# Moving one dt projection of a selective scan behind B's transposes, and giving VectorE two tiles of three groups of the last combine

## The chip, the cores and the metric

The kernel runs on one core of one Trainium2 chip. The metric is the time of one execution on the device, in microseconds (us), as the median of three runs.

## The reference

A macaron block on 16 sequences of 256 tokens with 128 features (4,096 tokens): half a mixture of experts (64 experts, the best 3 for each token, at most 64 tokens per expert), a selective scan (SSM) layer, and half a mixture of experts again with the same weights. Cut to what matters:

```python
x = x + 0.5 * ffn(layernorm(x))
x = x + ssm_layer(layernorm(x))
x = x + 0.5 * ffn(layernorm(x))

def ssm_layer(x):
    raw, gate = split(x @ W_in)
    h = silu(conv(raw, conv_w) + conv_b)
    ts, B, C = split(h @ W_x, [64, 80])
    dt = softplus(ts @ W_dt + b_dt)
    dA = exp(dt[..., None] * -exp(A_log))
    dBu = dt[..., None] * B[:, :, None, :] * h[..., None]
    state = dA_t * state + dBu_t          # over 256 times, 256 channels x 16 states
    y = sum_n(state * C)
    return ((y + h * D) * silu(gate)) @ W_out

def ffn(x):
    # gates of the best 3 experts; y = gelu(x w1 + b1) w2 + b2 of each expert's tokens
    out[token] += gate_k * y[row of (token, k)]    # k = 0, 1, 2
```

## The kernel before

All work is in float32 on tiles of 128 partitions. X, the tokens, stays in SBUF as 32 tiles of 128 tokens by 128 features. The order on each engine is written out by hand; engines wait for each other through semaphores that count events (wait(e, "dt", n) waits for the n-th dt).

**Scan.** The sequences are taken in eight blocks (q = 0 to 7) of two sequences. A block has 16 steps (n), one for each set of 32 channels by 4 state slots. For step n TensorE forms dBu by 64 small matmuls (dbu, L931), two steps ahead; ScalarE forms exp(dt·A) four steps ahead (decays, L1176); VectorE runs the recurrence (scan, L1307, three state buffers); GpSimd multiplies the states by C (times_c, L1386, seven product buffers); TensorE sums the products over the states (sum_states, L953). Between these steps the same queues do the work of other blocks: f = q + 2 is the front block, b = q + 1 the one behind it.

The front block's dt comes about so. x_parts (ScalarE, n = 11) copies ts and B, C out of PSUM. dt_proj(f, 0) and dt_proj(f, 1) (TensorE, L900, at n = 12) project ts to the two halves of 128 channels, into PSUM banks 6 and 7. softplus_rest(f, h) (ScalarE, L1132, L1134, L1136; n = 12 and 13) takes the absolute value, exp and ln. dt(f, 0) is formed by VectorE (L1292) at n = 15, dt(f, 1) at n = 0 of the next block. GpSimd's dtu (L1393) multiplies dt by h at n = 0 and 1 of the next block, each ahead of the product of that step. b_transposes(f) (TensorE, L889, n = 13) turns B, bt_copy(f) (ScalarE, L1143, n = 14) copies it to BT, and diagonal (VectorE, L1274, steps 0 and 1 of the next block; GpSimd L1401 and ScalarE L1160 too) spreads it to diagonal blocks for dbu. gates(b, 0) and gates(b, 1) (TensorE, L866, n = 15) write PSUM banks 6 and 7 again, and so wait for dt(f, 0) and dt(f, 1).

At q = 6 and 7 there is no front block. The blocks 0 and 1 of data are prepared ahead of the loop, in an order of its own that the change does not touch.

**Combine.** After the experts, y rows are read back from DRAM into YK by SP's queue, in PIECES of tiles, one read for each k (L394). TensorE multiplies each tile's rows by a diagonal of gates (gate_sums, L597, three k into one PSUM region), four tiles a group. The diagonals are formed by ScalarE among the experts (gate_diagonals, L424). In the second layer the fourth tile of each group is VectorE's instead (moe_residual, L743, three operations that depend on each other), and VectorE adds TensorE's three tiles to X (L748). SP stores X in OUT_PIECES.

## Time and profile before

| | us |
|---|---|
| median of 3 runs | 805.7 (802.46 to 810.35) |
| the profiled execution | 804.58 |
| its span, first to last instruction | 802.8 |
| busy in the span: TensorE, VectorE, ScalarE, GpSimd | 669.5, 595.5, 445.8, 490.5 |
| scan stretch | about 247 to 596 |
| combine of the second layer, reads issued to end | 775.1 to 802.8 |

The views that the prediction reads are these. The waits: for each engine and line, what ended its idle time, the total, how often and the longest. The timeline: instructions in order of time, neighbours of one line merged into a row. The chain: the work that ended last, followed back from the end. In a row of the timeline an instruction's name is the engine and the line of the kernel; neighbours of one engine overlap by up to 0.1 us, since the next starts before the end of the one before is recorded.

### The profile page before, as it was taken

Reading aid. Unit: us, or ns where it says so; the run is one execution under the profiler, and the core shown is the slowest. Engines: PE = TensorE matmul, PEld = TensorE weight load, DVE = VectorE, ACT = ScalarE, POOL = GpSimd, SP = SyncE. Lnnn points to the kernel's source line nnn. Section 1 sums busy time; section 2 is a strip of 40 time slices with the busy share of each in tenths; the row PEclk is TensorE's granted clock in tenths of the full one; section 3 lists DMA queues with packets and bytes.
Section 4 is the critical chain, followed back from the end, with each engine's and each line's share of the span. In section 5 each row is a group of like instructions: output and inputs, shape, how many; then the busy total and the mean of one; then the engine's idle time right before and its main releaser. Section 6 shows DMA issues by size and latency. Waiting matters only on the chain. (4 is left out here: it accounts for less than half of the span.)

```text
span 802.8 us, 27810 instructions
## 1 busy us (share of the span) xinstructions
PE 669.5 (83%) x11782; PEld 401.7 (50%) x11782; DVE 595.5 (74%) x1014; ACT 445.8 (56%) x925; POOL 490.5 (61%) x308
## 2 busy tenths in 40 slices
PE   6728989997978889989898989989989159999957
PEld 2615545555654445454454545454547035555547
DVE  7793443452698999999999999989999954434425
ACT  2400544452787888879798887877634004433420
POOL 3004555551038899999999999999961015555520
PEclk8758999999997999999999999999999579999979
DMA  8995898735283434453524245442009707997538
GB/s 271 397 341 172 290 315 308 234 112 213 117 185 80 98 103 112 124 120 96 147 53 122 73 122 121 123 108 56 4 3 341 288 10 265 323 330 248 168 114 320
DMA packets 87397, 141.07 MB, mean 176 GB/s; under 512 B 9779, under 2 KB 35005, under 8 KB 86000
## 3 DMA queue, kind: packets, MB, share of 16 engines
q1 hardware_dynamic: 82864, 126.99, 51.3%
q0 software_dynamic: 4416, 12.39, 4.1%
q8 instruction: 90, 1.47, 0.8%
q14 instruction: 27, 0.22, 0.1%
HBM read 112.02 MB, written 27.57 MB: 174 GB/s over the span
## 5 line engine op out<-in xcount | busy, mean ns | idle before, releaser
L1386 POOL TENSOR_TENSOR BIG<-BIG,R 128x1024 f32<-128x1024 f32 x127 | 305.5, 2440 | 12.4 <-DVE BIG L1307 12.2
L1307 DVE TENSOR_TENSOR_SCAN BIG<-BIG,ps 128x1024 f32<-128x1024 f32 x128 | 285.3, 2268 | 13.6 <-PE ps L931 10.9
L931 PE MATMUL ps<-BIG,stack 64*32 64x128 f32 x8192 | 155.9, 280 | 30.3 <-DVE BIG L1307 26.4
L931 PEld LDWEIGHTS ps<-BIG,stack 64*32 64x32 f32 x8192 | 118.5, 108 | 107.9 <-DVE BIG L1307 78.6
L767 POOL DMA_INDIRECT R<-xn_dram,tok_idx x64 | 65.4, 1021 | 89.9 <-DVE row_idx L700 70.9
L781 POOL DMA_INDIRECT y_dram<-BIG,row_idx x64 | 64.8, 1013 | 85.3 <-DVE BIG L724 41.7
L1176 ACT ACTIVATE BIG<-R,An 128x510 f32<-128x510 f32 x128 | 84.2, 710 | 5.2 <-DVE BIG L1307 5.1
L415 ACT ACTIVATE BIG<-BIG 128x512 f32<-128x512 f32 x64 | 40.2, 628 | 80.5 <-DVE BIG L716 69.7
L1176 ACT ACTIVATE BIG<-BIG,An 128x510 f32<-128x510 f32 x128 | 83.7, 708 | 0.2
L724 DVE COPY BIG<-ps 128x128 f32<-128x128 f32 x64 | 18.4, 288 | 82.7 <-remote 53.2
L409 ACT ACTIVATE BIG<-ps 128x128 f32<-128x128 f32 x64 | 17.0, 265 | 106.5 <-PE ps L533 71.7
L570 PE MATMUL ps<-BIG 128*64 128x128 f32 x960 | 70.2, 282 | 4.9 <-issue 4.9
L709 DVE COPY BIG<-ps 128x512 f32<-128x512 f32 x64 | 44.0, 688 | 35.5 <-PE ps L543 17.2
L953 PE MATMUL ps<-BIG,fold 128*32 128x512 f32 x512 | 69.4, 610 | 0.0
L543 PE MATMUL ps<-BIG 128*64 128x512 f32 x240 | 66.2, 630 | 0.8 <-ACT BIG L409 0.8
L553 PEld LDWEIGHTS ps<-ident,BIG 128*128 128x128 f32 x256 | 35.8, 209 | 53.7 <-issue 39.1
L570 PEld LDWEIGHTS ps<-BIG 128*64 128x64 f32 x960 | 53.8, 138 | 10.1 <-issue 5.8
L716 DVE TENSOR_TENSOR BIG<-ps,b1T 128x512 f32<-128x512 f32 x64 | 44.0, 688 | 13.3 <-remote 8.4
L1393 POOL TENSOR_TENSOR state_more<-state_more,BIG 128x512 f32<-128x512 f32 x16 | 26.4, 1648 | 43.5 <-DVE state_more L1292 43.5
L553 PE MATMUL ps<-ident,BIG 128*128 128x128 f32 x256 | 48.2, 311 | 1.5 <-DVE BIG L709 1.5
L424 ACT ACTIVATE BIG<-ident,gate 128x128 f32<-128x128 f32 (+1 forms) x112 | 38.0, 386 | 0.0
L1286 DVE SCALAR_TENSOR_TENSOR BIG<-ps,vcol,BIG 128x506 f32<-128x506 f32 (+2 forms) x48 | 34.8, 739 | 3.0 <-ACT BIG L1096 1.7
(184 smaller groups left out, 967.4 us busy)
## 6 DMA issues: line engine op xcount, KB each, us to landing
BIG<-in_L_ffn_w SPq DMA_DIRECT2D x120, 512.0 KB
BIG<-y_dram SPq DMA_DIRECT2D x18, 512.0 KB, 8.8
BIG<-dt_dram SPq DMA_DIRECT2D x32, 256.0 KB, 4.7
R<-c_dram SPq DMA_DIRECT2D x32, 256.0 KB, 7.2
R<-dt_dram SPq DMA_DIRECT2D x32, 256.0 KB, 5.0
y_dram<-zeros SPq DMA_DIRECT2D x3, 2048.0 KB, 16.9
y_dram<-zeros SPq DMA_DIRECT2D x24, 256.0 KB, 5.9
xn_dram<-R POOLq DMA_DIRECT2D x2, 2048.0 KB, 11.3
```

The source lines that it names most:

```text
L543: last = nc.tensor.matmul(ps[a * CAP:(a + 1) * CAP, 1 + s % 2, :], xt[s % 2][:, a * CAP:(a + 1) * CAP], w1s[b][:, a, :], start=True, stop= ...
L553: last = nc.tensor.transpose(ps[:, 3 + s % 2, c * P:(c + 1) * P], hs[s % 2].rearrange("n (p c) -> n c p", c=HC)[:, c, :], ident[:, :])
L570: last = nc.tensor.matmul(ps[a * CAP:(a + 1) * CAP, 5 + s % 2, 0:D], hT[s % 2][:, c, a * CAP:(a + 1) * CAP], w2s[b][:, a, c, :], start=Fal ...
L709: nc.vector.tensor_copy(hs[s % 2], ps[:, 1 + s % 2, :]).then_inc(S("hs"), 1)
L716: nc.vector.tensor_tensor(hb[s % 2].rearrange("p (c n) -> p c n", n=CAP), ps[:, 3 + s % 2, :].rearrange("p (c n) -> p c n", n=CAP), bias, ...
L767: nc.gpsimd.indirect_dma_start(xg[s], None, xn_dram[f], bass.IndirectOffsetOnAxis(tok_idx[:, j:j + 1].bitcast(U32), 0), bounds_check=T - 1 ...
L781: nc.gpsimd.indirect_dma_start(y_dram[f], bass.IndirectOffsetOnAxis(row_idx[:, j:j + 1].bitcast(U32), 0), yo[s], None, bounds_check=K * T ...
L931: last = nc.tensor.matmul(ps[CW * slot:CW * slot + CW, 2 * (st % 2) + b, :] .rearrange("p (g k s) -> p k g s", g=2, k=4)[:, k], dT[q % 2][ ...
L953: last = nc.tensor.matmul(ps[CW * j:CW * j + CW, 4 + h, :], fold32[:, :], prod[(st + j) % RP][:, :, g, :], start=False, stop=(gp == 1 and ...
L1176: last = nc.scalar.activation(dA[:, st % 6, :, g, 1:SEQ], dtR[h][:, j, :].rearrange("p (b t) -> p b t", b=2)[:, :, 1:SEQ], ACT.Exp, scale= ...
L1307: nc.vector.tensor_tensor_scan(state[st % 3], dA[:, st % 6].rearrange("p b g t -> p (b g t)"), ps[:, u:u + 2, :].rearrange("p b n -> p (b ...
L1386: nc.gpsimd.tensor_tensor(prod[st % RP], state[st % 3].rearrange("p (b g t) -> p b g t", b=2, g=2), Cf[q % 2][:, 2 * gp:2 * gp + 2].rearra ...
```

## The change

Two edits in the scan's order. TensorE issues dt_proj(f, 1) at step 14, behind dbu of that step, instead of at step 12. ScalarE copies B's transposes at step 13 and takes the second softplus at step 14, which were the other way round. What VectorE and GpSimd do at which step stays.

Three in the combine of the second layer. In groups 1, 3 and 5 VectorE takes the third tile too (BY_VECTOR), so TensorE has two there, and ScalarE forms no diagonals for them. For such a group VectorE first does k = 0 and 1 of both tiles and then adds TensorE's sum. The last eight tiles of y are read in two pieces of four (PIECES, in both layers), which is three DMA issues more on SP in each layer.

```diff
-PIECES = [(0, 4), (4, 8), (8, 16), (16, 24), (24, 32)]
+PIECES = [(0, 4), (4, 8), (8, 16), (16, 24), (24, 28), (28, 32)]
+BY_VECTOR = [(3,) if g % 2 == 0 or g == 7 else (2, 3) for g in range(8)]
+def vector_tiles(groups):
+    return sum(len(BY_VECTOR[g]) for g in range(groups))
...
-                if f == 1 and s % 4 == 3:
+                g = s // 4 + (2 * r if type(r) is int else 2)
+                if f == 1 and s % 4 in BY_VECTOR[g]:
                     return
...
-            tiles = 4 if f == 0 else 3
+            tiles = 4 if f == 0 else 4 - len(BY_VECTOR[g])
             if g == 0:
-                e.wait_ge(*S.at("gdiag", K * (NI if f == 0 else NI // 4 * 3)))
+                e.wait_ge(*S.at("gdiag", K * (NI if f == 0 else NI - vector_tiles(8))))
...
             for k in range(K):
-                if k:
-                    e.wait_ge(*S.at("x4", K * g + k))
-                nc.vector.scalar_tensor_tensor(out=X[:, i, :], in0=YK[:, k, i, :], scalar=gate[:, i, k:k + 1],
-                                               in1=X[:, i, :], op0=ALU.mult, op1=ALU.add).then_inc(S("x4"), 1)
-                if k == 0:
+                for m, t in enumerate(mine):
+                    i = 4 * g + t
+                    if k:
+                        e.wait_ge(*S.at("x4", K * vector_tiles(g) + len(mine) * (k - 1) + m + 1))
+                    nc.vector.scalar_tensor_tensor(out=X[:, i, :], in0=YK[:, k, i, :], scalar=gate[:, i, k:k + 1],
+                                                   in1=X[:, i, :], op0=ALU.mult, op1=ALU.add).then_inc(S("x4"), 1)
+                if k == len(mine) - 1:
                     e.wait_ge(*S.at("sum", g + 1))
-                    t = X[:, 4 * g:4 * g + 3, :].rearrange("p i d -> p (i d)")
-                    nc.vector.tensor_tensor(t, t, ps[:, g % 4, 0:3 * D], ALU.add).then_inc(S("x"), 1)
+                    t = X[:, 4 * g:4 * g + mine[0], :].rearrange("p i d -> p (i d)")
+                    nc.vector.tensor_tensor(t, t, ps[:, g % 4, 0:mine[0] * D], ALU.add).then_inc(S("x"), 1)
...
# TensorE, in the loop over steps
                             dt_proj(f, 0)
-                            dt_proj(f, 1)
                     if n == 13:
                         if run:
                             sum_states(q, 1, 0, 1)
                         if front:
                             b_transposes(f)
+                    if n == 14 and front:
+                        dt_proj(f, 1)
...
# ScalarE, in the loop over steps
                     if n == 13 and front:
+                        bt_copy(f)
+                    if n == 14 and front:
                         softplus_rest(f, 1)
-                    if n == 14 and front:
-                        bt_copy(f)
```

## Rows read from the trace of the kernel before

**Rows 1.** The waits, 250 to 597 us: engine, line, releaser, total, times, longest

```profile
DVE BIG L1307 <- PE ps L931: 10.9, 8, 2.3
```

**Rows 2.** Timeline of VectorE, block q = 2 and its end: start, length, instructions

```profile
367.87 6.63 DVE L1307 TENSOR_TENSOR_SCAN BIG<-BIG,ps 128x1024 f32<-128x1024 f32 x3
...
376.10 2.29 DVE L1307 TENSOR_TENSOR_SCAN BIG<-BIG,ps 128x1024 f32<-128x1024 f32 x1 [1.60 <-PE ps L931]
...
381.08 0.67 DVE L1292 SCALAR_TENSOR_TENSOR state_more<-ps,state_more 128x512 f32<-128x512 f32 x1
381.66 1.48 DVE L1274 TENSOR_TENSOR BIG<-fold,BT 128x1024 f32<-128x1024 f32 x1
383.07 2.27 DVE L1307 TENSOR_TENSOR_SCAN BIG<-BIG,ps 128x1024 f32<-128x1024 f32 x1
```

**Rows 3.** Timeline of TensorE, same stretch, and a lone projection (L861) later

```profile
372.92 1.98 PE L900 MATMUL ps<-BIG,Wdt 65*128 65x512 f32 x4
...
374.83 1.16 PE L931 MATMUL ps<-BIG,stack 64*32 64x128 f32 x64
...
377.27 2.33 PE L931 MATMUL ps<-BIG,stack 64*32 64x128 f32 x128
...
396.10 1.13 PE L861 MATMUL ps<-R,Wr 128*128 128x512 f32 x2
397.16 1.50 PE L931 MATMUL ps<-BIG,stack 64*32 64x128 f32 x64
```

**Rows 4.** Timeline of GpSimd, same stretch

```profile
363.68 14.03 POOL L1386 TENSOR_TENSOR BIG<-BIG,R 128x1024 f32<-128x1024 f32 x6
378.47 2.37 POOL L1386 TENSOR_TENSOR BIG<-BIG,R 128x1024 f32<-128x1024 f32 x1 [0.77 <-DVE BIG L1307]
...
382.02 3.36 POOL L1386 TENSOR_TENSOR BIG<-BIG,R 128x1024 f32<-128x1024 f32 x1
```

**Rows 5.** Timeline of GpSimd, blocks 6 and 7

```profile
544.53 51.58 POOL L1386 TENSOR_TENSOR BIG<-BIG,R 128x1024 f32<-128x1024 f32 x22
```

**Rows 6.** The chain that ended last, its end: start, length, what

```profile
786.70 12.34 PE ps L597 x108
799.06 0.56 DVE X L748
```

**Rows 7.** Timeline of ScalarE, block q = 2: first softplus's start, the second's passes

```profile
374.08 0.60 ACT L1132 ACTIVATE state_more<-ps 128x512 f32<-128x512 f32 x1 [1.57 <-PE ps L900]
...
377.13 0.58 ACT L1132 ACTIVATE state_more<-ps 128x512 f32<-128x512 f32 x1
...
378.41 0.63 ACT L1136 ACTIVATE state_more<-state_more 128x512 f32<-128x512 f32 x1
```

**Rows 8.** Timeline of VectorE, scans 12 and 17 of blocks 0 and 5

```profile
276.67 6.63 DVE L1307 TENSOR_TENSOR_SCAN BIG<-BIG,ps 128x1024 f32<-128x1024 f32 x3
...
291.40 2.27 DVE L1307 TENSOR_TENSOR_SCAN BIG<-BIG,ps 128x1024 f32<-128x1024 f32 x1
...
504.86 6.63 DVE L1307 TENSOR_TENSOR_SCAN BIG<-BIG,ps 128x1024 f32<-128x1024 f32 x3
...
519.59 2.27 DVE L1307 TENSOR_TENSOR_SCAN BIG<-BIG,ps 128x1024 f32<-128x1024 f32 x1
```

**Rows 9.** Timeline of GpSimd and VectorE, diagonals ahead of the scan

```profile
228.09 4.74 POOL L1401 TENSOR_TENSOR BIG<-fold,BT 128x1024 f32<-128x1024 f32 x2 [5.09 <-PE ps L597]
...
228.81 2.27 DVE L1274 TENSOR_TENSOR BIG<-fold,BT 128x1024 f32<-128x1024 f32 x1
```

**Rows 10.** Timeline of SP and VectorE, combine of the second layer

```profile
775.09 8.13 SPq L394 DMA_DIRECT2D BIG<-y_dram  x15
...
789.01 0.56 DVE L748 TENSOR_TENSOR X<-X,ps 128x384 f32<-128x384 f32 x1 [1.49 <-PE ps L597]
789.48 1.00 DVE L743 SCALAR_TENSOR_TENSOR X<-BIG,gate,X 128x128 f32<-128x128 f32 x3
...
799.53 0.73 DVE L743 SCALAR_TENSOR_TENSOR X<-BIG,gate,X 128x128 f32<-128x128 f32 x2
```

More of the change, by code:

```diff
@@ L736, in moe_residual @@
         def moe_residual(e, S, f, g):
-            i = 4 * g + 3
+            mine = BY_VECTOR[g]
             e.wait_ge(G(f"yk{PIECE[g]}"), 16 * K * (f + 1))
             for k in range(K):
-                if k:
-                    e.wait_ge(*S.at("x4", K * g + k))
-                nc.vector.scalar_tensor_tensor(out=X[:, i, :], in0=YK[:, k, i, :], scalar=gate[:, i, k:k + 1],
-                                               in1=X[:, i, :], op0=ALU.mult, op1=ALU.add).then_inc(S("x4"), 1)
-                if k == 0:
+                for m, t in enumerate(mine):
[5 more added lines that the diff above has]
+                if k == len(mine) - 1:
                     e.wait_ge(*S.at("sum", g + 1))
-                    t = X[:, 4 * g:4 * g + 3, :].rearrange("p i d -> p (i d)")
-                    nc.vector.tensor_tensor(t, t, ps[:, g % 4, 0:3 * D], ALU.add).then_inc(S("x"), 1)
+                    t = X[:, 4 * g:4 * g + mine[0], :].rearrange("p i d -> p (i d)")
+                    nc.vector.tensor_tensor(t, t, ps[:, g % 4, 0:mine[0] * D], ALU.add).then_inc(S("x"), 1)
         def moe_pool(e, S, LS, f):
@@ L1483, in _ @@
                 e.wait_ge(*F[1].at("x", i1 // 4))
-                e.wait_ge(*F[1].at("x4", K * i1 // 4))
+                e.wait_ge(*F[1].at("x4", K * vector_tiles(i1 // 4)))
                 ov = out.rearrange("(q b) (r j) d -> q (b r) (j d)", b=2, j=4)
```

## The prediction

> **What bounds the kernel now.** I read the waits of the scan stretch first, then one block of the scan on four engines, then the end of the program. In the scan (about 247 to 596 us) VectorE, GpSimd and TensorE are all close to full. Nearly all idle time of VectorE ahead of a scan is one wait, for TensorE's matmuls L931, 10.9 us in eight waits [rows 1]. Six of them are one per block of 16 steps in blocks q = 0 to 5, where work for a later block is still issued: ahead of the sixteenth scan of the block. In block q = 2 the scans of steps 12 to 14 end at 374.50 and the scan of step 15 starts at 376.10 [rows 2], because TensorE ran two dt projections (372.92 to 374.83) ahead of dbu(15) [rows 3]. The scan of step 15 followed the start of its dbu by 1.27 us. GpSimd does not idle as much: its products run from 363.68 without a gap to 377.71, and it waits 0.77 us for that late scan [rows 4]. In the last two blocks, without such work, GpSimd runs products back to back for 51.58 us (22 of them, 2.34 us each) [rows 5]; there the chain of work goes through GpSimd, so what the scan gains by block 5 must be a gain of GpSimd too, or it is lost.
>
> At the end TensorE is the bound: from 786.70 to 799.04 it forms the gate sums without a gap, 108 matmul records for 18 tiles, 0.68 us a tile, and VectorE follows each group [rows 6].
>
> **Part one, the moved projection.** A single projection of two matmuls of this size delays the next dbu by 1.06 us (396.10 to 397.16), the pair by 1.91 [rows 3]. So with one left in step 12, dbu(15) starts 0.85 earlier, at 373.98, and the scan of step 15 at 375.25: that stall falls from 1.60 to 0.75. TensorE then runs dbu(15), the sums, B's transposes and dbu(16) as before (2.43 us from dbu(15) to dbu(16), and 1.1 for dbu(16), half of 2.33 less the overlap) [rows 3]: 373.98 + 2.43 + 1.1 = 377.5 is where the second projection starts. dbu(17) is queued behind it and ends near 379.7; it is wanted only after 382. gates(b, 1) behind that waits for dt(f, 1) as it does now.
>
> ScalarE starts a softplus 1.16 us after its projection's start (372.92 to 374.08), and its three passes take 1.91 (377.13 to 378.41 + 0.63) [rows 7]. The second now ends at 377.5 + 1.16 + 1.91 = 380.6, where it ended at 379.04. The copy of B's transposes goes ahead of it for 0.1 and is ready in time: its first reader is the diagonal. VectorE would like to form dt(f, 1) at 376.10 − 0.85 + (381.08 − 376.10) = 380.23 and has it at 380.6: a new wait of 0.4, and 0.45 earlier than the 381.08 of before. The diagonal comes 0.58 later [rows 2], at 381.2.
>
> Then comes what decides. The diagonal and GpSimd's operations do not run side by side here: beside it a product takes 3.36 us where it takes 2.34 alone, and the scan behind the diagonal starts 1.05 after that product does (382.02, 383.07) [rows 2, 4]. GpSimd's row is fixed: products of steps 9 to 14 to 377.68, then the product of step 15 without its wait of 0.77, then dt·u, then the product of step 16; from the one product to the other it was 382.02 − 378.47 = 3.55, so 381.23 now. If the diagonal is issued by then, it takes its turn between the two, and scan 17 starts at 381.23 + 1.05 = 382.28 instead of 383.07. Measured from the start of scan 12 that is 14.41 where block 2 has 15.20. The six blocks have 14.73, 15.07, 15.20, 14.73, 14.98 and 14.73 (first and last in [rows 8]), in sum 89.44; six times 14.41 is 86.46. The scan gains 3.0 us, and it cannot gain more, since 14.41 is GpSimd's own row. At block 5 GpSimd has gained the same, and the last two blocks pass it on.
>
> The margin is thin: 381.2 against 381.23 in block 2. Where the stall was shorter, the projection comes earlier against scan 12, so the room is 0.03 + (15.20 − the distance): 0.5 in blocks 0, 3 and 5, 0.25 in block 4, 0.16 in block 1, 0.03 in block 2. Where the diagonal comes too late, it waits for a whole product: 2.33 us for that block. At the scan's beginning, when GpSimd started first on such a diagonal, VectorE's took 2.27 us, against 1.1 with the turn free [rows 9]. I take the turn as caught in all six, which the sum favours by a hair in one of them.
>
> The Trainium skill (SBUF — State Buffer, "SBUF: two separate sides") says the same and speaks against moving anything close to such an edge: a VectorE operation with two SBUF inputs and a GpSimd operation hold their common ports as an exclusive lock for a whole instruction. By that rule a late diagonal costs a whole product; by the row of 2.27 a wait of about 1.2 is shown, with the other end unseen.
>
> **Part two, the second layer's combine.** VectorE takes one more tile in groups 1, 3 and 5: nine operations more on VectorE, nine matmuls (18 records) fewer on TensorE, nine diagonals fewer on ScalarE, which has gaps among the experts (nothing counted). Group 1 is done before the data of group 2 are there at 786.70, so two tiles count: 2 × 0.68 = 1.36 us. VectorE must follow. Three of its operations on one tile take 1.00, two that depend on each other 0.73 [rows 10], which gives 0.35 for one, a distance of 0.38 if it depends on the one before and 0.27 if not; the addition takes 0.47. A group of one own tile is then 0.27 + 0.47 + 0.38 + 0.27 = 1.4, one of two tiles 4 × 0.27 + 0.37 (two thirds of the width, estimated) + 2 × 0.27 = 2.0. A sum is taken up 0.27 after TensorE's last tile of it (786.70 + 3 × 0.68 = 788.74, addition at 789.01). From there 1.13, 2.0 and 0.27 bring the addition of group 4 to 792.4 (TensorE after 8 tiles 792.14, ready at 792.4), another 3.4 that of group 6 to 795.8 (13 tiles, ready at 795.8), and that of group 7, wanted at 797.2, waits for TensorE until 799.06 − 1.36 = 797.7. So 1.3 us come off, with VectorE a tie away from being the bound.
>
> The last read in two pieces adds three issues on SP's queue in each layer. Fifteen take 8.13 us, 0.54 each [rows 10]; three more end the issuing at 784.8, ahead of the first store, and in layer one ahead of the next DMA that waits on the front of the scan. TensorE now wants tiles 24 to 27 at 793.4 and 28 to 31 at 795.4. All of the last read was there when it was used at 794.7; its first half, issued first, should be there earlier. Not shown is what smaller packets (2 KB for 4) do to the rate. From below I bound it by nothing, from above by the whole 1.3; I take nothing, because a half in hand replaces a whole.
>
> Sum: 3.0 + 1.3 = 4.3. The profiled execution (span 802.8, time 804.58) would come to a span of 798.5; it lay 1.1 below the median of 805.7. From the median: 805.7 − 4.3 = 801.4.
>
> **The rivals.**
> One block late: only block 2 loses its turn, 801.4 + 2.3 = 803.7.
> Several late (the other side): the second softplus ends 0.2 us or more later than reckoned and two to six blocks lose it. Two cost 4.7 and wipe out 4.3; blocks 1, 2 and 4 give 801.4 + 7.0 = 808.4; all six, past 0.5 us, 815.4. For it speaks the thin margin, against it that three blocks have 0.5.
> The scan gains nothing: the earlier scan 15 is paid back by the wait for dt, and only the combine is left, 805.7 − 1.3 = 804.4. GpSimd's 0.77 of idle time speaks against it.
> The combine gains nothing: data or VectorE come last there, 805.7 − 3.0 = 802.7.
> That the change does nothing at all is the sum of these two, and small.
>
> **How the numbers follow.** Forecast 0.42, one block late 0.20, several late 0.13, no gain in the scan 0.10, no gain in the combine 0.15. All but the worst of these lie between 801.4 and 808.4; the three runs of before spread over 8 us, so I add 3 below: 798.5 to 808.5. One per cent, 8 us, is about what a measurement of this kernel can tell from no change. Faster by more would need more than both parts can give: 0.05. Slower by more is all six blocks late: 0.05. Within 1%: 0.90.
>
> **What the changed profile would show.** VectorE's wait for L931 ahead of scan 15 near 0.3 to 0.75 instead of 1.1 to 1.6; a new wait of VectorE for ScalarE's L1136 pass of some 0.4; GpSimd without a wait ahead of the product of step 15; scan 17 at 14.4 after scan 12 in all six blocks. A diagonal of over 2 us would show a lost turn. In the end: the last addition 1.3 us closer to the start of group 2's sums, and no wait for y's reads in groups 6 and 7. The prediction is wrong if two or more blocks have a long diagonal, or if GpSimd's row from block to block isn't what sets 14.4.

## The result, and the profile after

| | before | after |
|---|---|---|
| median on the same chip, four runs each | 804.1 us (799.35 to 810.35) | 816.5 us (810.25 to 818.87) |
| the profiled execution, its span | 804.58, 802.8 | 818.87, 817.1 |
| first scan to the end of the last | 355.7 | 374.3 |
| last combine: first read issued to the end of VectorE's last operation | 25.2 | 25.1 |

The changed kernel is slower: the ratio is 1.0135 (95% interval 1.0086 to 1.0184). Every ratio here and below compares the runs that lie within 1.5% of their kernel's fastest. The forecast was 801.4 us, with a range up to 808.5. In the two profiles the scan stretch alone is 18.7 us longer. It began 4.7 us earlier than in the profile of before, so the span grew by 14.3. The earlier start is variation: the one edit that reaches the part ahead of the scan is the split of the first layer's last read, and in the profiles below the scan starts at 223.6 to 227.5 us with that split and at 225.1 to 230.0 without it, all where the kernel before takes 783 us.

First the groups of instructions (line, engine, operation, names, shapes, count | busy us, mean ns | idle before). This is VectorE's diagonal in the kernel after, over the whole span. Before, the first diagonal of a block took 1.48 or 1.49 us in all six blocks (1.48 in [rows 2]):

```profile
L1285 DVE TENSOR_TENSOR BIG<-fold,BT 128x1024 f32<-128x1024 f32 x16 | 40.5, 2537 | 0.1
```

The same block-to-block piece as in [rows 2], here block q = 1, timeline of VectorE (start, length, instructions, idle before):

```profile
319.70 6.63 DVE L1318 TENSOR_TENSOR_SCAN BIG<-BIG,ps 128x1024 f32<-128x1024 f32 x3
326.61 2.29 DVE L1318 TENSOR_TENSOR_SCAN BIG<-BIG,ps 128x1024 f32<-128x1024 f32 x1 [0.27 <-PE ps L941]
...
331.97 0.69 DVE L1303 SCALAR_TENSOR_TENSOR state_more<-ps,state_more 128x512 f32<-128x512 f32 x1 [0.30 <-ACT state_more L1147]
332.58 5.17 DVE L1285 TENSOR_TENSOR BIG<-fold,BT 128x1024 f32<-128x1024 f32 x1
337.67 2.27 DVE L1318 TENSOR_TENSOR_SCAN BIG<-BIG,ps 128x1024 f32<-128x1024 f32 x1
```

Up to the diagonal all goes about as forecast: scan 15 follows scan 12 by 6.9 us (7.25 by the prediction's working, 8.10 before), the wait for L941 is 0.27, and the new wait for softplus 0.30. The diagonal is issued 12.88 us after scan 12. Then it takes 5.17 us. GpSimd over the same time, as in [rows 4]:

```profile
315.51 16.35 POOL L1397 TENSOR_TENSOR BIG<-BIG,R 128x1024 f32<-128x1024 f32 x7
331.83 1.27 POOL L1404 TENSOR_TENSOR state_more<-state_more,BIG 128x512 f32<-128x512 f32 x1
333.06 2.38 POOL L1397 TENSOR_TENSOR BIG<-BIG,R 128x1024 f32<-128x1024 f32 x1
335.39 1.28 POOL L1404 TENSOR_TENSOR state_more<-state_more,BIG 128x512 f32<-128x512 f32 x1
340.02 5.67 POOL L1397 TENSOR_TENSOR BIG<-BIG,R 128x1024 f32<-128x1024 f32 x2 [3.36 <-DVE BIG L1318]
```

The diagonal was issued at 332.58, 0.48 ahead of the boundary at 333.06. GpSimd's product of step 16 went first all the same, at 2.38 us undisturbed, and its second dt·u after that. VectorE's turn came at 336.7, when GpSimd had nothing ready (its next product needs scan 17, which was queued behind the diagonal). TensorE's timeline shows what that brings after it:

```profile
334.86 1.07 PE L963 MATMUL ps<-BIG,fold 128*32 128x512 f32 x8
340.00 1.96 PE L941 MATMUL ps<-BIG,stack 64*32 64x128 f32 x64 [4.07 <-DVE BIG L1318]
341.89 1.93 PE L963 MATMUL ps<-BIG,fold 128*32 128x512 f32 x8
```

The stretches around it (us, then busy time and records of TensorE, its weight loads, VectorE, ScalarE, GpSimd; granted clock of TensorE, DMA share, GB/s):

```profile
330.00:339.30 9.30, 5.34 (x140) 2.44 (x140) 9.00 (x4) 8.98 (x20) 6.66 (x4) 1.00 0.26 88
339.30:346.10 6.80, 6.10 (x127) 3.72 (x134) 6.17 (x5) 1.94 (x5) 5.61 (x2) 0.50 0.01 2
346.10:360.00 13.90, 13.19 (x328) 7.21 (x310) 13.58 (x10) 10.18 (x20) 11.72 (x5) 1.00 0.75 172
```

TensorE goes without work for 4.07 us, and from 3.4 us into that gap it is granted 0.50, that is 1.2 GHz, for 6.8 us; the matmuls of a step take 1.96 us there and 1.16 at full clock. So a lost turn costs more than itself.

All six blocks, in us after the start of each block's scan 12, from the starts in the timelines of both kernels:

| block | scan 17 before | scan 17 after | diagonal issued | its length | next block's scan 12, later by |
|---|---|---|---|---|---|
| 0 | 14.73 | 16.68 | 13.51 | 3.25 | 2.31 |
| 1 | 15.07 | 17.97 | 12.88 | 5.17 | 4.36 |
| 2 | 15.20 | 16.77 | 13.45 | 3.39 | 1.57 |
| 3 | 14.73 | 18.00 | 12.88 | 5.20 | 3.55 |
| 4 | 14.98 | 16.73 | 13.85 | 2.96 | 1.72 |
| 5 | 14.73 | 17.94 | 13.27 | 4.75 | 3.61 |

The last column sums to 17.1, and block 6, which has no diagonal of the loop but has 3.4 us of TensorE at 0.50 near its start, adds 1.5. That is the 18.7 us. Scan 17 itself accounts for 14.7 of it; the rest lies behind it.

There are two kinds of block. In 0, 2 and 4 the diagonal is issued after GpSimd's product 16 has begun (13.28 to 13.39), and it waits for that product: scan 17 at 16.7. In 1, 3 and 5 it is issued ahead of that start, and yet waits for both the product and the dt·u behind it: scan 17 at 18.0. The first kind is the prediction's rival of late diagonals. The second was in no case of it. The prediction's own sign of being wrong, two or more long diagonals, is there in all six blocks.

The waits of VectorE over the scan stretch, 250 to 610 us, against [rows 1]:

```profile
DVE BIG L1318 <- PE ps L941: 6.6, 8, 2.2
DVE state_more L1303 <- ACT state_more L1147: 2.9, 6, 0.7
DVE BIG L1310 <- PE ps L963: 2.3, 5, 0.8
```

The wait that the change was to shorten fell from 10.9 to 6.6. VectorE's wait for its turn with GpSimd ("the port" below, as in the prediction's common ports) stands in no row of waits: it is counted as busy time of the diagonal.

### The profile page after: what moved, and what is told of

Read it like the earlier page. It is cut to its first block, busy times and chain, and to the rows that moved or that the text cites. A ratio compares the mean times of both kernels' runs of the same rounds, so it can differ in the third digit from the quotient of the medians.

```text
span 817.1 us, 27772 instructions
## 1 busy us (share of the span) xinstructions
PE 671.1 (82%) x11764; PEld 398.4 (49%) x11764; DVE 615.0 (75%) x1023; ACT 444.1 (54%) x916; POOL 486.9 (60%) x308
## 4 chain that ended last, share of the span: by engine, by line
PE 56%; DVE 23%; issue 7%; another core or an unknown queue 4%; ACT 4%; DMA 3%; SPq 1%; POOL 0%; DVEq 0%; ACTq 0%; POOLq 0%
PE ps L941 14%; DVE BIG L1318 8%; PE ps L551 6%; PE ps L578 6%; PE ps L963 5%; PE ps L561 4%; PE ps L605 3%; PE ps L910 2%; DMA BIG<-y_dram 2%; PE ps L885 2%; PE ps L876 2%; PE ps L985 1%; PE ps L519 1%; PE ps L871 1%
## 5 line engine op out<-in xcount | busy, mean ns | idle before, releaser
L941 PE MATMUL ps<-BIG,stack 64*32 64x128 f32 x8192 | 157.1, 281 | 48.7 <-DVE BIG L1318 41.2
L941 PEld LDWEIGHTS ps<-BIG,stack 64*32 64x32 f32 x8192 | 118.7, 108 | 128.1 <-DVE BIG L1318 87.1
L963 PE MATMUL ps<-BIG,fold 128*32 128x512 f32 x512 | 72.8, 639 | 0.5 <-DVE BIG L1328 0.5
L578 PEld LDWEIGHTS ps<-BIG 128*64 128x64 f32 x960 | 53.3, 137 | 10.9 <-issue 6.8
L1404 POOL TENSOR_TENSOR state_more<-state_more,BIG 128x512 f32<-128x512 f32 x16 | 23.5, 1467 | 43.8 <-DVE state_more L1303 43.8
L1285 DVE TENSOR_TENSOR BIG<-fold,BT 128x1024 f32<-128x1024 f32 x16 | 40.5, 2537 | 0.1
```

The source lines that it names most:

```text
L578: last = nc.tensor.matmul(ps[a * CAP:(a + 1) * CAP, 5 + s % 2, 0:D], hT[s % 2][:, c, a * CAP:(a + 1) * CAP], w2s[b][:, a, c, :], start=Fal ...
L941: last = nc.tensor.matmul(ps[CW * slot:CW * slot + CW, 2 * (st % 2) + b, :] .rearrange("p (g k s) -> p k g s", g=2, k=4)[:, k], dT[q % 2][ ...
L963: last = nc.tensor.matmul(ps[CW * j:CW * j + CW, 4 + h, :], fold32[:, :], prod[(st + j) % RP][:, :, g, :], start=False, stop=(gp == 1 and ...
```

## The experiments

Most of them ran where the kernel before takes 783 us, so the ratios to that kernel, run beside them, are what is compared; the last ran where it takes 803. The runs of other sequences of the two engines and the one with the read in one piece were executed once each. A "lost turn" is a boundary between two of GpSimd's operations that passes while VectorE's diagonal is already waiting and does not let it in.

### Which part of the change, and which engine's part

**The scan's edits alone, and the combine's alone.** Each is the kernel before with one half of the diff that stands ahead of the prediction.

> Only the scan's two order edits on the kernel before; the combine is as before. Theory P (VectorE's first diagonal loses its turn on the port it shares with GpSimd, by one or two GpSimd operations in each of the six blocks): 11 to 14 us above the kernel before, diagonals of 2.9 to 5.2 us in blocks 0 to 5. Theory C (the combine or its extra reads cost most of it): within 2 us of the kernel before. Theory D (the new wait of VectorE for the second softplus, 0.3 to 0.7 us a block, is the loss by itself): 2 to 4 us above.

> Only the combine's edits (two tiles of three groups, last read in two pieces). Theory P: no loss, 0 to 1.3 us below the kernel before. Theory C: 5 us or more above it. The forecast's term for this part was 1.3 us less.

Scan edits: ratio 1.0105 (1.0073 to 1.0137), the scan 367.5 us, diagonals of 2.87, 5.16, 3.41, 1.60, 5.14 and 1.59. Combine: 0.9969 (0.9941 to 0.9997), the scan 356.1, first diagonals of 1.49 or 1.50. The loss is the scan's, though at 8 us it is less than the 11 to 14 expected. And blocks 3 and 5 of the first run are what was forecast: the diagonal issued at 12.87 takes 1.60, scan 17 follows at 14.39, and block 3 takes 45.08 us. Blocks 1 and 4 lost two turns, with the same times up to the diagonal. The first diagonals of blocks 3 and 4:

```profile
423.10 1.60 DVE L1275 TENSOR_TENSOR BIG<-fold,BT 128x1024 f32<-128x1024 f32 x1
...
468.20 5.14 DVE L1275 TENSOR_TENSOR BIG<-fold,BT 128x1024 f32<-128x1024 f32 x1
```

VectorE's starts up to the diagonal agree within 0.02 us in the four blocks, and GpSimd's product of step 16 comes at 13.29 to 13.35 in all. So nothing that these times show tells a block with a lost turn from one without.

**TensorE's half and ScalarE's half of the scan's edits.**

```diff
                             dt_proj(f, 0)
-                            dt_proj(f, 1)
...
+                    if n == 14 and front:
+                        dt_proj(f, 1)
```

```diff
                     if n == 13 and front:
-                        softplus_rest(f, 1)
+                        bt_copy(f)
                     if n == 14 and front:
-                        bt_copy(f)
+                        softplus_rest(f, 1)
```

> The kernel before, with only TensorE's part of the change: the second dt product at step 14, ScalarE's order as it was (second softplus at step 13, copy of B's transposes at step 14). The sums of step 13 come ahead of the product, so scan 15 should start 6.9 to 7.5 us after scan 12. Theory P (scan 16 that ends before GpSimd's first dt·u begins costs VectorE's diagonal its turns): most blocks lose one or two turns, diagonals of 3 to 5 us, ratio 1.007 to 1.016. Theory S (it is ScalarE's new order that does the harm): diagonals of 1.5 us and a ratio of at most 1.002.

> The kernel before, with only ScalarE's part: the copy of B's transposes at step 13, the second softplus at step 14. TensorE's order is left as it was, so scan 15 still starts 7.7 to 8.3 us after scan 12, scan 16 still ends after GpSimd's first dt·u has begun. Theory P: no lost turn, diagonals of 1.5 us, the same time (ratio 0.997 to 1.003). Theory S: VectorE waits for the late softplus in each block, its diagonals come later, the ratio is over 1.005.

The product's move alone: 1.0190 (1.0149 to 1.0231), more than the 1.016 expected at most. Four blocks lose two turns or one more than fair, scan 17 at 17.9; VectorE also waits 0.65 us a block for the copy of B's transposes, now behind the late softplus. ScalarE's order alone: 0.9992 (0.9964 to 1.0020), all diagonals 1.48 or 1.49. The move of the product does the harm; ScalarE's new order is harmless by itself, and with it the loss is smaller (1.0105).

**The second product one step later instead of two.**

```diff
-                            dt_proj(f, 1)
                     if n == 13:
                         ...
                             b_transposes(f)
+                            dt_proj(f, 1)
```

> The kernel before, with the second dt product moved one step later instead of two: at step 13, right behind B's transposes; ScalarE's order is left as it was. The sums of step 13 are then ahead of the product, as in the changed kernel, so scan 15 should start 7.0 us after scan 12 (before: 7.7 to 8.2). Theory P: the gain of scan 15 alone brings scan 16's end to before GpSimd's first dt·u begins, so product 16 is ready at that boundary and VectorE's diagonal loses its turn in most blocks: diagonals of 3 to 5 us, blocks of 47 us and more, ratio 1.005 to 1.015 against before. Theory D (it is the late softplus, two steps behind): with the product one step later VectorE waits less than 0.2 us for softplus and the ratio is 0.997 to 1.002.

Ratio 1.0076 (1.0019 to 1.0133), but only five of the ten runs are within 1.5% of the fastest and count in it; the median of all ten is 794.8 against 783.3, 1.5% more. The profiled run, of 797.6 us, has diagonals of 4.75, 4.49, 3.10, 3.12, 3.10 and 4.85, and VectorE never waits for softplus in it. The ten times range from 783.2 to 801.7 us, where the kernel before has 776.8 to 789.7. I take that as a number of lost turns that differs from one execution to the next; with one profile it isn't shown.

### Is it the port

**Diagonals that read PSUM.** In the blocks from the third on VectorE's diagonals take B's transposes from PSUM, where TensorE wrote them, so one operand instead of two is in SBUF. TensorE's skip product waits until they are done. The same edit was made to both kernels.

```diff
+                turned = ps[:, 4, NS * k:NS * k + NS] if b >= 2 else BT[:, k, :]
-                                        BT[:, k, :].unsqueeze(2).broadcast_to([P, NS, 64]), ALU.mult)\
+                                        turned.unsqueeze(2).broadcast_to([P, NS, 64]), ALU.mult)\
```

> The changed kernel, with one edit: in the blocks from the third on, VectorE's two diagonals read B's transposes from PSUM (where TensorE wrote them) and not from their copy in SBUF, so each has one operand in SBUF where it had two. For that TensorE must not write over the bank until the diagonals are done: its skip product waits for them. Theory P (the lost microseconds are turns that VectorE loses to GpSimd when both of an operation's inputs are in SBUF): no diagonal from the third block on takes over 1.3 us (1.19 is the least seen in the changed kernel), GpSimd's products beside them go back to about 2.4 us, scan 17 starts 13.9 to 14.2 us after scan 12 (16.7 to 18.0 in the changed kernel, 14.7 to 15.2 in the one before), the scan is at or below the 355.7 us of the kernel before, and the time is the same as before or up to 6 us under it. Theory D (the delay comes with the move itself: the late softplus and the second dt product hold back scan 15 and what follows, whatever the diagonals do): the diagonals get short but the blocks stay over 47 us, and the ratio stays above 1.008. A third outcome, from the run with the diagonals at steps 7 and 8: the stall goes to TensorE, here through its wait ahead of the skip product, and half the loss stays (ratio near 1.005).

> The kernel before, with the same one edit: VectorE's diagonals read B's transposes from PSUM from the third block on. Theory P: the wait for the port is all that the edit takes away, and in the kernel before it is small: a diagonal goes from 1.49 to 1.20 us, scan 17 comes 0.3 us earlier in each of six blocks, and GpSimd's product beside it goes from 3.4 to 2.4 us; the time is 0 to 4 us under that of before. Theory D: the same as before within 1 us. If PSUM as the source, or TensorE's new wait, costs something of its own, it shows here, as blocks over 45.9 us.

In the changed kernel with this edit:

```profile
L1288 DVE TENSOR_TENSOR BIG<-fold,ps 128x1024 f32<-128x1024 f32 x12 | 14.4, 1203 | 0.0
```

Twelve diagonals of 1.20 us each, ratio 0.9975 (0.9941 to 1.0008), the scan 357.7 us instead of 374.3. Nearly the whole loss was VectorE's wait for the port. The scan is not at or below the 355.7 of before, as expected: scan 17 comes at 14.4 to 14.9 in blocks 1 to 5 and not at 13.9 to 14.2, with scan 15 at 7.3 to 7.6 and not at 6.9. In the kernel before the edit does nothing that can be measured (1.000, 0.997 to 1.003), though every first diagonal fell from 1.49 to 1.21: there the turn cost 0.3 us.

**The diagonals somewhere else.** VectorE's diagonals right behind the scans of steps 7 and 8, and, in another run, the first diagonal ahead of the second dt.

```diff
-                    if n - (3 if q == 0 else 0) in (0, 1) and back:
-                        diagonal(b, n - (3 if q == 0 else 0))
+                    if n in (7, 8) and back:
+                        diagonal(b, n - 7)
```

```diff
-                    if q >= 1 and n == 0 and back:
-                        dt(b, 1)
                     if n - (3 if q == 0 else 0) in (0, 1) and back:
                         diagonal(b, n - (3 if q == 0 else 0))
+                    if q >= 1 and n == 0 and back:
+                        dt(b, 1)
```

> The changed kernel with VectorE's two diagonals of a block issued right behind the scans of steps 7 and 8 of the block before, where GpSimd runs dry and waits for VectorE, instead of at steps 0 and 1. Theory P: every diagonal near 1.1 to 1.2 us, GpSimd's dt-u and products at their own 1.27 and 2.35, and the time below the kernel before by 3 us or more (the 11 to 14 are gone, the shorter stall of step 15 remains, and 2.3 us a block of blocked port is gone). Theory D: the wait for the second softplus stays, and so does most of the loss: 8 us or more above the kernel before.

> The changed kernel with VectorE's first diagonal ahead of dt(b, 1) and not behind it, so that it asks for the port when the scan of step 16 ends, 0.3 to 0.7 us earlier plus the 0.6 of dt itself. Theory P, by which the turn depends on asking before GpSimd's next operation is ready: GpSimd's product of step 16 becomes ready by the same scan, so VectorE asks at the same time or before, gets the port after dt-u in all blocks, diagonals below 1.8 us, and the time is within 2 us of the kernel before. Theory D: VectorE's idle time for dt only shrinks by the diagonal, the rest of the loss stays, 8 us or more above.

At steps 7 and 8 no turn was lost (1.20 each), but the ratio stayed 1.0121 (1.0092 to 1.0150) and the blocks took 46.4 to 47.9 us. By the number this is theory D's case, 8 us or more. TensorE's timeline shows another stall, here in block 0:

```profile
307.85 1.44 PE L941 MATMUL ps<-BIG,stack 64*32 64x128 f32 x64 [2.60 <-DVE BIG L1318]
```

TensorE now went without work for 2.2 to 2.6 us there in blocks 0, 1, 2 and 4, so this run says nothing for or against the port: I had expected it to. With the diagonal first, four runs took 793.1, 794.8, 806.9 and 816.6 us, the last with a granted clock of 0.81 over the run where the others have 0.92; they are too far apart for a ratio. All are 10 us or more above the kernel before, where theory P had at most 2. In the profiled one, of 793.1 us, five diagonals took 1.37 to 2.07 us, and one block (4.89 us, issued at 11.88) lost its turns again. In these two runs, moving the operation moved the stall.

### Who gets a turn

**The two engines alone.** Two programs without the kernel: GpSimd runs products of 128x1024, VectorE asks once for a product with both inputs in SBUF. In the first, six products in a row, with and without fulfilled waits. In the second, the kernel's sequence (product, dt·u, a product that VectorE releases, dt·u, products) with the release and the asking moved across the start of dt·u in steps of 0.1 us.

> Nothing of the reference: 36 trials in which GpSimd issues six products of 128x1024 in a row (both inputs in SBUF) and VectorE, once the third has ended, runs zero, one or two copies out of PSUM (128x512) and then asks for one product of 128x1024 with both inputs in SBUF. Modes: GpSimd's products without a wait between them; with a wait that is long fulfilled; with a wait that ScalarE fulfils only after the product before has ended. The output is zeros. Theory P (GpSimd keeps the turn where its next operation is ready at a boundary): in the first two modes VectorE's product waits for all the remaining products of the six, or for a varying number of them, so 4 to 9 us; in the third it gets in at the first boundary, under 4 us. Theory of fair turns (the prediction's): never more than one product's rest (2.0 us) above its own 1.2 us, in any mode.

> Nothing of the reference, the output is zeros: 102 trials of the kernel's sequence at the boundary of blocks. GpSimd: a product of 128x1024, a dt·u of 128x512 in place, a product that waits for VectorE's 'scan', a second dt·u, two products. VectorE, at the same time: copies out of PSUM of 960 to 2496 columns in steps of 96 (0.1 us), the 'scan' (a copy of 512 columns that releases the product), none, one or two more copies, then one product with both inputs in SBUF, whose time is read. So the release falls from about 0.7 us before the first dt·u begins to 1 us behind it. Theory P: where the release falls behind the start of dt·u, VectorE's product takes at most the rest of dt·u and its own 1.2 us (under 2.5 us); where it falls ahead of it, it often loses one or two turns (3.4 to 5.2 us). Theory of fair turns: never over the rest of the running operation plus 1.2 us, on either side; then what takes the turns in the kernel is something that these engines alone don't show.

My theory, in this form, fell. In all 36 trials of the first and all 102 of the second VectorE got the first boundary behind its asking: 2.14 to 3.36 us in the first program, at most 2.32 in the second where it asked ahead of the product behind dt·u, up to 3.40 where it asked behind that product's start. Where the release fell made no difference.

So I went back to the kernels. Nine profiles (before, after, the halves and parts of the diff alone, the product one step later, the diagonal ahead of dt, and the combine with one read, below) have 54 such block ends. In 36 of them GpSimd's product of step 15 starts within 0.11 us of the end of scan 15, that is, GpSimd had waited for it, as in [rows 4]. None of these lost a turn: in 28 VectorE asked ahead of product 16 and got the boundary, in eight it asked behind that product's start and waited for its end. In 18 the product starts 0.23 to 0.60 us after scan 15's end, so GpSimd was behind and did not wait for it: thirteen of these lost one or more. In twelve of the thirteen VectorE was let in 16.8 to 16.9 us after scan 12, at the end of dt·u, when GpSimd ran dry; in the other, the diagonal ahead of dt, also where GpSimd had nothing ready. Those 18 have nine of GpSimd's operations in a row without a pause ahead of dt·u, 20.5 us. This was sorted after the fact, so it gives a theory and not a test.

**Long rows.** Two programs with rows of products, each released by a "scan" of VectorE whose last part (its columns) sets the pace: with wide ones GpSimd keeps step with the releases, with narrow ones it is released ahead.

> Nothing of the reference, the output is zeros: 64 trials. GpSimd: rows of 2, 5, 8 or 11 products of 128x1024, each released by a 'scan' of VectorE, then a dt·u of 128x512, a product released by one more scan, a second dt·u, a product. VectorE: the scans (four operations on PSUM and SBUF, together 2.1 to 2.5 us, by the width of the last: 512, 400, 300 or 200 columns), a dt of 512 columns, the last scan, a second dt, then the product with both inputs in SBUF whose time is read. With narrow scans GpSimd falls behind and runs the row without a pause, with wide ones it pauses before every product. Theory R (an unbroken row takes the turns): VectorE's product takes 3.4 us and more in trials of 8 and 11 products with narrow scans, whenever it asks ahead of the product behind dt·u, and at most 2.5 us in the others. Fair turns: it gets the first boundary after its asking in all 64.

> Nothing of the reference, the output is zeros: 120 trials as in the run with rows of 2 to 11 products, now with 5, 8, 11, 14 and 20 products and a last scan operation of 300, 200, 120 or 40 columns, six times each. Theory R (an unbroken row of GpSimd's operations that are released ahead takes the turns): with 11 and more products and 200 columns or fewer, VectorE's product loses one turn or more (3.4 us and more although it asked ahead of the boundary) in a good part of the trials, in rows of 5 in none, and at 300 columns (GpSimd's product released just as the one before it ends) in none. Rival (a rare event whatever the row): losses are as rare in the long rows as before, 0 to 3 in 120.

The first had one loss in 64, three turns, in a row of eleven, so theory R failed there as it was stated: rows of eight and the other three of eleven with narrow scans lost none. The second, trials with a loss, of six each:

| products in the row | 300 columns | 200 | 120 | 40 |
|---|---|---|---|---|
| 5 | 0 | 0 | 0 | 0 |
| 8 | 0 | 0 | 0 | 0 |
| 11 | 0 | 2 | 0 | 3 |
| 14 | 0 | 5 | 3 | 6 |
| 20 | 0 | 6 | 6 | 6 |

Two trials of 14 products and 200 columns, VectorE's operation first, then GpSimd; the first got its turn, the second didn't:

```profile
4177.33 1.98 DVE L81 TENSOR_TENSOR vc<-va,vb 128x1024 f32<-128x1024 f32 x1
```

```profile
4144.62 32.38 POOL L42 TENSOR_TENSOR c<-a,b 128x1024 f32<-128x1024 f32 x14 [2.42 <-DVE fill L64]
4176.97 1.25 POOL L43 TENSOR_TENSOR d<-d,a 128x512 f32<-128x512 f32 x1
4178.19 3.31 POOL L46 TENSOR_TENSOR c<-a,b 128x1024 f32<-128x1024 f32 x1
```

```profile
3429.85 7.44 DVE L81 TENSOR_TENSOR vc<-va,vb 128x1024 f32<-128x1024 f32 x1
```

```profile
3396.80 32.37 POOL L42 TENSOR_TENSOR c<-a,b 128x1024 f32<-128x1024 f32 x14 [2.42 <-DVE fill L64]
3429.14 1.26 POOL L43 TENSOR_TENSOR d<-d,a 128x512 f32<-128x512 f32 x1
3430.37 2.33 POOL L46 TENSOR_TENSOR c<-a,b 128x1024 f32<-128x1024 f32 x1
3432.66 1.25 POOL L47 TENSOR_TENSOR d<-d,a 128x512 f32<-128x512 f32 x1
3433.88 2.33 POOL L48 TENSOR_TENSOR c<-a,b 128x1024 f32<-128x1024 f32 x1
```

A product that VectorE's got in ahead of reads 3.31, its own 2.33 and the wait. In the second trial none of GpSimd's is longer than alone, and VectorE's 7.44 us end 1.1 us behind the last of them (3436.2): it was let in when the row was over. This is what block 1 of the changed kernel shows. It takes a long row: five and eight products never lost a turn, however far ahead they were released. That it takes operations released ahead as well isn't shown by the column of 300: there VectorE asked within 0.03 us of the boundary and took 1.22 us, so it never stood waiting at one. For that half there are only the kernel's blocks above and the last run below.

### Breaking the row in the kernel

**GpSimd waits for both dt.** Its first dt·u waits for the second dt, so that it pauses where VectorE asks.

```diff
-                wait(e, "dt", 2 * b + h + 1)
+                wait(e, "dt", 2 * b + 2 if b >= 2 else 2 * b + h + 1)
```

> The changed kernel, with one edit: in the blocks from the third on, GpSimd's first dt·u waits for VectorE's second dt (12.96 us after scan 12) where it waited for the first (9.8). GpSimd then pauses about 0.8 us, VectorE asks for the port in that pause. Theory P (turns lost at the port are the loss): VectorE's diagonal takes 1.2 to 1.5 us in every block where scan 15 started at 6.9, scan 17 starts 13.9 to 14.3 us after scan 12, the blocks are 45.0 to 46 us and the ratio against before is 0.993 to 1.002. Rival: GpSimd, 0.6 us later with its products than in the kernel before, becomes what TensorE's sums and so the scans wait for; then the diagonals are short, but the blocks are over 46.5 us and the ratio over 1.005.

The first diagonal takes 1.21 or 1.22 us in every block and scan 17 comes at 14.0 in blocks 1 to 4, but GpSimd, a microsecond and a half behind, now makes the second diagonal wait (2.45), and TensorE waits for its dt·u. Blocks 1 to 4 take 45.9 to 46.4 us, ratio 1.0058 (1.0027 to 1.0088): about half of the loss is gone, and the rival is half right (the ratio, not the blocks of over 46.5 us).

**A wait of 0.1 us.** The changed kernel, with GpSimd's product of step 15 also waiting for the first dt, which ends just about when that product would start by itself.

```diff
                     if 0 <= STEPS * q + n < STEPS * NQ - 1:
+                        if n == 15 and q + 2 < NQ:
+                            wait(e, "dt", 2 * q + 5)
                         times_c(STEPS * q + n)
```

> The changed kernel, with one edit: GpSimd's product of step 15 also waits for VectorE's first dt, which ends 9.77 us after scan 12, where the product starts by itself at 9.74 to 9.84. So GpSimd has to wait for a semaphore once ahead of dt·u, for 0.1 us at most. Theory R (an unbroken row takes the turns): VectorE gets the first boundary behind its asking in every block; diagonals of 1.6 us where scan 15 started at 6.9, scan 17 at 14.4, blocks of 45.1 to 45.7 us, no block over 47, the scan at 353 to 356 us (changed kernel 374.3, before 355.7), and a ratio of 0.990 to 0.998 against before. If the lost turns are not due to the unbroken row, diagonals of 4.7 us and more stay in half of the blocks and the ratio stays above 1.007. In between: the row is broken, but asks that come behind the start of product 16 (13.3 us) still wait for its end, fairly, with a loss of 1.7 us each in up to three blocks; ratio 0.997 to 1.004.

GpSimd and VectorE in block 2 of that kernel:

```profile
361.95 14.04 POOL L1397 TENSOR_TENSOR BIG<-BIG,R 128x1024 f32<-128x1024 f32 x6
376.14 2.38 POOL L1397 TENSOR_TENSOR BIG<-BIG,R 128x1024 f32<-128x1024 f32 x1 [0.15 <-DVE state_more L1303]
378.47 1.27 POOL L1404 TENSOR_TENSOR state_more<-state_more,BIG 128x512 f32<-128x512 f32 x1
379.70 3.35 POOL L1397 TENSOR_TENSOR BIG<-BIG,R 128x1024 f32<-128x1024 f32 x1
```

```profile
379.16 1.66 DVE L1285 TENSOR_TENSOR BIG<-fold,BT 128x1024 f32<-128x1024 f32 x1
380.75 2.27 DVE L1318 TENSOR_TENSOR_SCAN BIG<-BIG,ps 128x1024 f32<-128x1024 f32 x1
```

With 0.15 us of waiting the diagonal takes its turn at the boundary, as [rows 2] had it. In blocks 3 and 4 the wait is too short for the profile to show it as idle time. Block 4, seven products and dt·u:

```profile
452.40 16.40 POOL L1397 TENSOR_TENSOR BIG<-BIG,R 128x1024 f32<-128x1024 f32 x7
468.76 1.27 POOL L1404 TENSOR_TENSOR state_more<-state_more,BIG 128x512 f32<-128x512 f32 x1
```

The row reads 16.40 us where block 1 of the changed kernel has 16.35, and the product of step 15 starts at 9.85 and not at 9.79, 0.08 behind the end of the dt that it waits for. The turn is kept there too. Five of six diagonals take 1.65 to 1.67; the sixth was issued at 13.43, 0.04 behind the product's start, and waits for it, fairly (3.42). Scan 17 comes at 14.45 to 14.60 in blocks 1 to 4, those blocks take 45.14 to 45.29 us where the kernel before has 45.42 to 45.88, and the scan is 357.1 us. The ratio is 0.9984 (0.9950 to 1.0019). One wait on a semaphore in each block takes back what the change cost. It isn't measurably faster than before, and the scan missed the 353 to 356 us expected: the 1.9 us that blocks 1 to 4 gain go again in block 0 (1.1, its scan 15 comes late at 8.25) and block 5 (1.7, the late diagonal). This kernel and the one with diagonals that read PSUM both have the combine's edits in them, which alone give 0.9969. So no run here shows a gain from the moved projection, even with its turns kept.

### The combine

**The last eight tiles read in one piece**, with VectorE's second tiles kept.

```diff
-PIECES = [(0, 4), (4, 8), (8, 16), (16, 24), (24, 28), (28, 32)]
+PIECES = [(0, 4), (4, 8), (8, 16), (16, 24), (24, 32)]
```

> The combine part of the change alone, but the last eight tiles read in one piece as before. If the split read is what brought the y rows 0.7 us later (TensorE's first wait for y at group 2: 12.3 us after the first read was issued, before 11.6), the group-2 sums start 11.6 us after the issue here, and the end of the last addition comes 24.1 to 24.6 us after the issue (before 25.2, after 25.1). If the reads are late by chance or by VectorE's other order, 12.3 stays.

Group 2's sums start 12.5 us after the first read's issue, in the run with the split read 12.9, in the changed kernel 12.3, before 11.6. The split isn't what makes the rows late, and the other profiles say that nothing in the edit is: 11.4 to 11.9 in six with the old combine, 11.1 to 12.9 in eight with VectorE's tiles. From the addition of group 2 to the last one it is 10.05 us before, 9.63 with VectorE's tiles alone, and 9.19 to 9.23 in seven profiles with the split as well. So each half of the edit is worth 0.4 us. TensorE's sums in the kernel after, groups 2 and 4, the first rows of each:

```profile
801.83 0.49 PE L605 MATMUL ps<-BIG,R 128*128 128x128 f32 x2 [1.22 <-DMA BIG<-y_dram]
...
805.68 0.49 PE L605 MATMUL ps<-BIG,R 128*128 128x128 f32 x2 [0.23 <-DMA BIG<-y_dram]
```

The second wait is new: the five tiles of groups 2 and 3 are done before the next rows are there. In all eight profiles with VectorE's tiles, group 4's sums start 3.83 to 3.87 us behind group 2's, however late those are, and with the read in one piece group 6's, another 3.77 behind, wait too (0.16). VectorE at the end of that stretch (before, each addition from group 2 on waited 0.54 us or more for TensorE; here only those of groups 2, 4 and 7 wait):

```profile
811.34 0.56 DVE L758 TENSOR_TENSOR X<-X,ps 128x384 f32<-128x384 f32 x1
811.81 1.00 DVE L753 SCALAR_TENSOR_TENSOR X<-BIG,gate,X 128x128 f32<-128x128 f32 x3
813.35 0.55 DVE L758 TENSOR_TENSOR X<-X,ps 128x384 f32<-128x384 f32 x1 [0.54 <-PE ps L605]
```

The combine's edits alone have the lowest ratio of all, 0.9969 (0.9941 to 0.9997): faster than the kernel before by 0.3%. The intervals of the two kernels with 0.9975 and 0.9984 overlap with it.

## Why the prediction was wrong, step by step

- **Scan 15 earlier, softplus later.** Right in kind. The wait ahead of scan 15 was forecast at 0.3 to 0.75 and measured at 0.27 to 0.82; the new wait for softplus at 0.4, and measured at 0.30 in blocks 1 to 3 and 0.65 to 0.67 in 0, 4 and 5. GpSimd's boundary was at 13.28 to 13.39, where 13.36 was forecast. The diagonal was asked for at 12.88 in blocks 1 and 3, and at 13.27 to 13.85 in the others.
- **"If the diagonal is issued by then, it takes its turn between the two".** This is the step that failed. In blocks 1, 3 and 5 it was issued 0.48, 0.45 and 0.06 us ahead and took 5.17, 5.20 and 4.75 us, with scan 17 at 18.0 and not at 14.41. It was read off blocks in which GpSimd had waited 0.3 to 0.8 us for scan 15 a moment before [rows 4]. The change took away that very wait, which I counted as a gain, and with it what had kept the turns fair. The run with a wait of 0.15 us or less put back shows that the step holds as long as the row is broken. Why an unbroken row takes the turns, and why only sometimes, stays open.
- **The room of 0.03 to 0.5 us.** Too thin by its own reckoning, and this rival was right in its mechanism and its price. Blocks 0, 2 and 4 asked 0.06 to 0.48 us too late; scan 17 came at 16.7 where 14.41 + 2.33 = 16.74 was forecast for a late one. The room came out as -0.23, 0.48, -0.06, 0.45, -0.48 and 0.06 in blocks 0 to 5, where 0.5, 0.16, 0.03, 0.5, 0.25 and 0.5 were forecast. Part of it is the longer wait for softplus, part a scan 15 that came later in blocks 2 and 4 (7.48 and 7.42, against 6.90). Both follow a block with lost turns, so the margins may depend on each other; it isn't a rule, since block 5 of the scan's edits alone follows one too, at 6.90. The rival's time for all six late, 815.4, is close to the 816.5 measured, but by luck: three of its six turns were lost in another way, at 3.5 us each.
- **"The scan gains 3.0 us."** Even with the turns kept it is less. With the row broken, blocks 1 to 4 gain 1.9 together where 2.3 was forecast for them, and in the one profile of that kernel the first and the last give more than that back.
- **The combine, 1.3 us.** Right in kind, too large: 0.84 by the timeline, from group 2's addition to the last. TensorE remains the bound there, but the 1.36 counted for its two tiles overlooked a wait: I asked whether the last read would be in time, and not the one before it. TensorE's first tile of group 4 starts 0.4 us later than the tiles before it would allow and takes 0.1 longer, which is the missing 0.5. The last read's split, taken as nothing, is worth 0.4 of the 0.84. The time with this part alone, 2.4 us less (0.2 to 4.6), includes both figures.
- **The chances.** I gave 0.05 to slower by over 1%, for six late blocks as one event. Six blocks whose margins vary by 0.4 us and more from one to the next are six draws and not one event, and the spread of the run one step later, 783 to 802 us from the same program, fits that.

The Trainium skill (SBUF — State Buffer, "SBUF: two separate sides") has the pair as an exclusive lock for a whole instruction that the one starting first gets. The traces agree that the loser waits for the whole instruction: asked for just behind the start of a product of 2.33 us, VectorE's operation of 1.2 takes up to 3.40. The Trainium skill also says, under "Who interferes with whom", "Issue order, not op shape, decides who blocks." The order alone doesn't decide here. In the two trials of 14 products shown above VectorE asks ahead of the same product of GpSimd's, which has long been released; one gets in at 1.98 us and the other at 7.44. In block 1 of the changed kernel the diagonal was issued 0.48 us ahead of the start of GpSimd's product of step 16 and 2.8 ahead of that of the second dt·u, and both went first. The measurement decides.

## What to carry to other kernels

An idle gap of a neighbour can be what keeps two engines' turns at a shared port fair; before closing it, ask which operation with two SBUF inputs waits for a turn behind the row that becomes unbroken. In this kernel nine operations of GpSimd in a row were enough. Such a wait shows as a long busy operation, not as idle time, so compare the longest of a group with its shortest. If it appears, give the waiting engine's operation one operand in PSUM, or let the busy engine wait for a semaphore that is fulfilled about then: a wait of 0.15 us or less in each block bought back the 1.35% here.

## What the hardware showed that I had not expected

- VectorE's operation with two SBUF inputs can be passed over by GpSimd for as long as GpSimd has released work: 3 turns after 14 products (7.4 us for an operation of 1.2), 5 turns after 20 (11.4 us, asked 3.2 us ahead of dt·u). No row of eight or fewer did this in any trial; in the kernels a row of nine operations did, in 13 of 18 blocks. What counts, the number of operations or the time they run, these runs don't separate, nor why nine, eleven and fourteen do it only sometimes; that stays open.
- GpSimd's recorded operations stay at 2.33 us while VectorE is passed over, and read 3.3 when VectorE gets in between: the wait is recorded at the one that waits.
- TensorE was granted 0.50 of its clock for 6.8 us around a gap of 4.07 us, and the same matmuls took 1.96 instead of 1.16 us. In block 3 a gap of 4.11 us came with 3.4 us of it.
